# Attention of a gated layer on one core: two Q/K and value buffers, products spread over the heads, weight copies on GpSimd

## What is computed

```python
# 16 heads of 32
scores = einsum("bqhd,bkhd->bhqk", q, k) / sqrt(32); probs = softmax(where(causal, scores, min))
attn = einsum("bhqk,bkhd->bqhd", probs, v).reshape(b, s, d) @ Wo.T
mod = 0.1 * tanh(attn @ A)                       # rank 16
gate = silu(h @ W_in.T + mod * (h @ A) @ B)
out = hidden + (gate * (h @ W_up.T)) @ W_down.T
x = x + tanh(g_ffn) * out
```

## Time and profile before

| | |
|---|---|
| median of 3 runs | 1079.77 us (1079.33 to 1080.65) |
| the profiled execution | 1080.39 us |
| its span | 1078.7 us |
| TensorE matmuls, busy | 1035.0 us (96%) |
| TensorE weight loads | 860.9 us (80%) |
| VectorE | 735.5 us (68%) |
| ScalarE | 613.1 us (57%) |
| GpSimd | 177.7 us (16%) |
| mean granted TensorE clock | 0.997 |

### The profile page before, as it was taken

One profiled execution on the slowest core, in us unless ns is written; L12 is line 12 of the kernel. 1 busy time (PEld: TensorE's weight loads), 2 busy tenths in 40 slices (PEclk: granted clock), 3 DMA queues, 4 the chain that ended last, 5 costly groups with the idle time before them and its releaser, 6 DMA issues.

```text
span 1078.7 us, 17949 instructions
## 1 busy us (share of the span) xinstructions
PE 1035.0 (96%) x5336; PEld 860.9 (80%) x5337; DVE 735.5 (68%) x1662; ACT 613.1 (57%) x1463; POOL 177.7 (16%) x156
## 2 busy tenths in 40 slices
PE   6999999999999999989999999999999999899998
PEld 6787878777888888878888888778888877788887
DVE  7766747996665559985664589966655689854443
ACT  4464547886444458875444378864354588754342
POOL 4536122320000003320000024200000133200000
PEclk9899999999999999999999999999999999999999
DMA  6534132443322425243322354432234342333221
GB/s 244 188 141 165 39 118 70 97 100 120 105 88 90 151 69 140 64 119 128 108 89 88 108 142 97 112 117 88 88 102 141 85 121 68 79 91 105 88 88 49
DMA packets 47063, 115.59 MB, mean 107 GB/s; under 512 B 6800, under 2 KB 6800, under 8 KB 46096
## 3 DMA queue, kind: packets, MB, share of 16 engines
q1 hardware_dynamic: 43968, 105.06, 33.1%
q0 software_dynamic: 3040, 9.96, 2.7%
HBM read 76.46 MB, written 13.37 MB: 83 GB/s over the span
## 4 chain that ended last, share of the span: by engine, by line
PE 80%; DVE 9%; issue 3%; DMA 3%; ACT 2%; SPq 1%; POOL 1%; DVEq 0%; ACTq 0%; POOLq 0%
PE bank L510 64%; PE bank L709 4%; PE bank L722 3%; DVE wr L1326 3%; DVE nb L1338 3%; PE bank L681 3%; DMA stack<-wr 2%; PE bank L758 1%; SPq L307 1%; DVE big L1347 1%; PE bank L685 1%; ACT big L962 1%; PE bank L769 1%; PE bank L566 1%; DMA big<-in_x,gidx 1%
## 5 line engine op out<-in xcount | busy, mean ns | idle before, releaser
L510 PE MATMUL bank<-hT,wr 128*128 128x512 f32 x1488 | 358.4, 390 | 0.0
L510 PEld LDWEIGHTS bank<-hT,wr 128*128 128x128 f32 x1488 | 278.9, 188 | 59.9 <-issue 1.3
L510 PE MATMUL bank<-wr,actr 128*128 128x512 f32 (+1 forms) x1224 | 303.3, 397 | 2.2 <-DVE actr L1308 1.5
L510 PEld LDWEIGHTS bank<-wr,actr 128*128 128x128 f32 x1224 | 229.1, 190 | 51.1 <-issue 3.3
L1376 DVE SCALAR_TENSOR_TENSOR wr<-stream,lns,wr 128x256 fp32r<-128x256 f32 x256 | 122.3, 538 | 51.0 <-ACT wr L1001 51.0
L1326 DVE TENSOR_TENSOR wr<-bank,wr 128x512 fp32r<-128x512 f32 (+1 forms) x224 | 124.6, 600 | 19.7 <-ACT wr L878 19.7
L962 ACT ACTIVATE big<-bank,nb 128x512 f32<-128x512 f32 (+3 forms) x256 | 131.7, 531 | 9.7 <-DVE nb L1338 8.2
L878 ACT ACTIVATE actr<-act_sb 128x512 fp32r<-128x512 f32 x64 | 40.4, 632 | 145.7 <-DVE act_sb L1390 145.7
L878 ACT ACTIVATE wr<-bank 128x512 fp32r<-128x512 f32 (+1 forms) x224 | 102.6, 532 | 27.8 <-PE bank L510 18.7
L1013 ACT ACTIVATE sil<-bank 128x512 f32<-128x512 f32 x64 | 38.1, 596 | 137.6 <-PE bank L758 137.6
L485 POOL TENSOR_SCALAR big<-big,rr 128x256 f32<-128x256 f32 x64 | 78.0, 1219 | 205.9 <-DVE rr L1343 205.9
(11 more groups left out here) (182 smaller groups left out, 1078.6 us busy)
## 6 DMA issues: line engine op xcount, KB each, us to landing
stream<-in_wmlp SPq DMA_DIRECT2D x64, 512.0 KB, 4.0
stack<-wr SPq DMA_DIRECT2D x192, 128.0 KB, 2.3
stream<-in_wmlp SPq DMA_DIRECT2D x64, 256.0 KB, 2.7
big<-in_x SPq DMA_DIRECT2D x4, 1024.0 KB, 5.5
big<-y_rows SPq DMA_DIRECT2D x4, 1024.0 KB, 5.6
residual<-big SPq DMA_DIRECT2D x4, 1024.0 KB, 5.1
big<-residual SPq DMA_DIRECT2D x4, 1024.0 KB, 5.6
out<-big SPq DMA_DIRECT2D x3, 1024.0 KB, 4.5
```

Of the source, the lines that this page charges most:

```text
L510: mm = pe.matmul(dst, lhs(pl, k), rhs(pr, k), start=start and i == 0, stop=stop and i == n - 1, skip_group_check=skip)
```

## The change

- `qk` and `vst` have two buffers, taken by q modulo 2. The high half of Q waits for the stack DMAs of two quads back. In `vst` the high and low halves of two heads lie side by side without zeros, so `attend` loads 48 columns of weights in place of 64, and a memset of the tile goes.
- Each of heads 0 to 8 has six projection products: those of K of quad 1 are half ahead of the loop, and then come Q and K of the later quads by halves.
- Q of quad 1 is split ahead of the loop. In it K of quad q + 1 is split at j = 1, and Q of quad q + 2 at j = 3 of quads 0 and 1. The values of quad q + 1 are split at j = 2 of quad q, those of quad 0 at head 0.
- The weights of quads 2 and 3 are copied by GpSimd (`weights_high`), a projection of 512 columns at a time, and its subtraction follows each copy. ScalarE still copies those of quads 0 and 1 ahead.
- The first up product is spread over heads 9 to 14, two matmuls each, behind `attend`.
- Scores wait for the exponentials bank by bank.
- K of quad 0 goes to bank 3 and the value products of tiles 2 and 3 to bank 6, so that bank 7 can be cleared (the matmul with `zeror`) before the first scores. The last transposes of head 0 wait until bank 6 is read out.
- The loops over quads are written out on every engine.

```diff
@@ -91,11 +93,14 @@
-qk = carve(6144, 2048).rearrange("p (m t) -> p m t", m=4)
-pts = carve(8192, 4 * PACKED).rearrange("p (h a c) -> p h a c", h=2, a=2)
-VS = QH * 64 + 64
-vst = carve(8192 + 4 * PACKED, TT * VS).rearrange("p (t c) -> p t c", t=TT)
-vst_v = vst[:, :, 0:QH * 64].rearrange("p t (h c) -> p t h c", h=QH)
+qk = carve(6144, 4096).rearrange("p (n m t) -> p n m t", n=2, m=4)
+pts = carve(10240, 4 * PACKED).rearrange("p (h a c) -> p h a c", h=2, a=2)
+VS = QH * 2 * R
+vst = carve(10240 + 4 * PACKED, 2 * TT * VS).rearrange("p (n t c) -> p n t c", n=2, t=TT)
+vst_v = vst.rearrange("p n t (g s c) -> p n t g s c", g=2, s=2)
+vp_v = flat[:, 6656:6656 + TT * H * R].rearrange("p (t g c) -> p t g c", t=TT, g=H // 2)
...
@@ -415,6 +420,16 @@
+    def weights_high(b, q, which):
+        pool.wait_ge(qk_done, (b * NQ + q - 1) * 2 + which + 1)
+        g.tensor_copy(wqs[:, HI, which, :, :], wqk_v[:, which, :, q * P:q * P + P]).then_inc(wq_hi, 1)
+    def weights_low(b, q, which):
+        pool.wait_ge(wq_hi, (b * NQ + q) * 2 + which + 1)
+        g.tensor_tensor(wqs[:, LO, which, :, :], wqk_v[:, which, :, q * P:q * P + P],
+                        wqs[:, HI, which, :, :].bitcast(F32), ALU.subtract).then_inc(wq_lo, 1)
...
@@ -485,18 +491,20 @@
-        weights_low(b, 1)
+        for which in range(2):
+            weights_low(b, 1, which)
         normalise(b * H)
         for q in range(NQ):
             for j in range(QH):
                 if q < NQ - 1 or j < QH - 1:
                     normalise((b * NQ + q) * QH + j + 1)
-                if j == 1 and q < NQ - 2:
-                    weights_low(b, q + 2)
+                if j < 2 and q < NQ - 2:
+                    weights_high(b, q + 2, j)
+                    weights_low(b, q + 2, j)
         if b < NB - 1:
-            weights_low(b + 1, 0)
+            for which in range(2):
+                weights_low(b + 1, 0, which)
...
@@ -655,12 +663,10 @@
-            pe.wait_ge(wq_hi, n + 1)
-            pe.wait_ge(wq_lo, n + 1)
-            if which and to == QKB:
-                pe.wait_ge(qk_lo, n * 2 + 1)
+            pe.wait_ge(wq_lo, n * 2 + which + 1)
+            if q:
+                pe.wait_ge(qk_lo, n * 2 + which)
...
@@ -685,17 +688,24 @@
+        if not first:
+            pe.wait_ge(exp_ok, n * 4 - 3)
         rows(3, True)
         mask(0, 3 * P, 1)
+        if not first:
+            pe.wait_ge(exp_ok, n * 4 - 1)
         rows(2, True)
         rows(0, False)
         mask(1, 2 * P, 2)
+        if not first:
+            pe.wait_ge(exp_ok, n * 4)
         rows(1, True)
         mask(2, P, 1)
-    def turn_probs(n, par, first=False):
+    def turn_probs(n, par, first=False, values_out=0):
...
@@ -719,35 +732,35 @@
-                mm = pe.matmul(bank[ATT][0:64, kt * P:S], vst[:, kt, 64 * j:64 * j + 64],
+                at_row = 64 * (j // 2) + R * (j % 2)
+                mm = pe.matmul(bank[ATT][0:3 * R, kt * P:S], vst[:, q % 2, kt, at_row:at_row + 3 * R],
                                pts[:, j % 2, part, at:at + w], start=False, stop=False, skip_group_check=True)
         mm.then_inc(pv_done, 1)
-    def head_step(b, q, j, ahead):
+    def head_step(b, q, j):
         n = (b * NQ + q) * QH + j
-        if j == 2 and ahead == 2:
-            project(b, q + 2, 0, half=0)
-        if j == 0 and ahead:
-            project(b, q + 1, 1)
-        if j == 3 and ahead == 2:
-            project(b, q + 2, 0, half=1)
-        if ahead or j < QH - 1:
+        head = q * QH + j
+        if j == 0 and q < NQ - 1:
+            project(b, q + 1, 1, half=1)
+        elif j and q < NQ - 2:
+            project(b, q + 2, (0, 0, 1)[j - 1], half=(0, 1, 0)[j - 1])
+        if head < H - 1:
             turn_probs(n + 1, (j + 1) % 2)
-        if not ahead and j < QH - 1:
-            if j == 0:
+        if head < H - 3:
+            m = b * (H // 2) + q * 2 + (j + 3) // 2
+            scores(n + 3, (j + 1) % 2, m * 48 + 48)
+        attend(b, q, n, j)
+        if UP_FROM <= head < H - 1:
+            if head == UP_FROM:
                 pe.wait_ge(qk_lo, (b + 1) * (NQ * 2))
                 pe.wait_ge(cg_hi, b * NCH + 1)
                 pe.wait_ge(cg_lo, b * NCH + 1)
-            up_part(0, ((0,), (1,), (2, 3))[j])
-        if ahead or j < QH - 3:
-            m = b * (H // 2) + q * 2 + (j + 3) // 2
-            scores(n + 3, (j + 1) % 2, m * 48 + 48)
-        attend(b, q, n, j)
+            up_part(0, head - UP_FROM)
...
@@ -821,18 +837,12 @@
-        turn_probs(b * H, 0, first=True)
+        turn_probs(b * H, 0, first=True, values_out=b + 1)
         scores(b * H + 2, 0, b * (H // 2) * 48 + 96)
-        pe.wait_ge(vpb_ok, b + 1)
-        pe.matmul(bank[ATT][:, :], zeror[:, :], hT[:, HI, 0, :], start=True, stop=False,
-                  skip_group_check=True).then_inc(pv_done, 1)
-        with pe.Fori(0, NQ - 2) as q:
+        project(b, 1, 1, half=0)
+        for q in range(NQ):
             for j in range(QH):
-                head_step(b, q, j, 2)
-        for q, ahead in ((NQ - 2, 1), (NQ - 1, 0)):
-            for j in range(QH):
-                head_step(b, q, j, ahead)
+                head_step(b, q, j)
...
@@ -968,30 +979,32 @@
-    def head_step(b, q, j, ahead):
+    def values_high_of(b, q):
+        if q < 2:
+            act.wait_ge(vpa_ok, b + 1)
+            act.wait_ge(vpb_ok, b + 1)
+        else:
+            act.wait_ge(pv_done, b + 1 + (b * NQ + q - 1) * QH)
+        copy(vst_v[:, q % 2, :, :, HI, :], vp_v[:, :, 2 * q:2 * q + 2, :]).then_inc(vst_hi, 1)
+    def head_step(b, q, j):
         n = (b * NQ + q) * QH + j
-        if ahead or j < QH - 1:
+        if q < NQ - 1 or j < QH - 1:
             exponentials(n + 1, (j + 1) % 2)
             normalise(n + 1, (j + 1) % 2)
-        if j < 2 and ahead:
-            split_qk(b, q + 1, j)
+        if j == 1 and q < NQ - 1:
+            split_qk(b, q + 1, 1)
+        elif j == 3 and q < NQ - 2:
+            split_qk(b, q + 2, 0)
         for i, (bk, w, at) in enumerate(((4, 512, 0), (5, 512, 512), (6, 256, 1024))):
             act.wait_ge(p_turned, n * 3 + i + 1)
             copy(pts[:, j % 2, HI, at:at + w], bank[bk][:, 0:w]).then_inc(pt_hi, 1)
-        if j == 0:
-            act.wait_ge(pv_done, b + 1 + n)
-            act.wait_ge(vpa_ok, b + 1)
-            act.wait_ge(vpb_ok, b + 1)
-            act.wait_ge(vst_zero, 1)
-            copy(vst_v[:, :, :, 0:R], vp[:, :, bass.ds(q * QH, QH), :]).then_inc(vst_hi, 1)
-    def quad(b, q, ahead):
-        for j in range(QH):
-            head_step(b, q, j, ahead)
-            if j == 1 and ahead == 2:
-                split_wqk(b, q + 2)
+        if q == 0 and j == 0:
+            values_high_of(b, 0)
+        elif j == 2 and q < NQ - 1:
+            values_high_of(b, q + 1)
...
@@ -1467,14 +1480,14 @@
+        qk_low(b, 1, 0)
         maxima(b * H + 1)
         dve.wait_ge(vp_done, b * 2 + 2)
         v.tensor_copy(vp[:, 2:4, :, :].rearrange("p t h r -> p (t h r)"),
                       bank[VALUES[1]][:, :]).then_inc(vpb_ok, 1)
-        with dve.Fori(0, NQ - 2) as q:
-            quad(b, q, 2)
-        quad(b, NQ - 2, 1)
-        quad(b, NQ - 1, 0)
+        for q in range(NQ):
+            for j in range(QH):
+                head_step(b, q, j)
```

96 lines of the change are left out of this document (48 added, 48 removed).

## The result

The changed kernel takes 1064.55 us (median of 4 runs, 1063.31 to 1066.72), the kernel before, on the same chip, 1079.55 (4 runs, 1077.52 to 1080.65). The ratio is 0.9867, with a 95% interval of 0.9854 to 0.9879: faster by 15.0 us, where 1063.0 was forecast. The profiled execution took 1066.72, span 1064.6.

What follows compares the result with a forecast made beforehand. VectorE was taken as the fullest engine in the attention loop, with 3.3 us a batch of waits. Terms 1.06 + 0.94 + 0.65 + 0.60 - 0.22 + 1.15 = 4.2 a batch, some 17 in four, gave 1063.0 us, range 1058.5 to 1071.

Steps and rivals of the forecast that it cites:

- the forecast's own case: Whole kernel: 1060 to 1067 us, the summed gains halved or full; chance 0.60.
- 3.3 us a batch is waiting on VectorE: Attention loop, head 1's to head 15's reciprocal: VectorE's work fills 64.9 of 68.2 us, the rest is waits.
- The second Q/K buffer: First heads of quads 1 and 2: removes two 0.53 waits for ScalarE's Q copy, held by stack DMAs; 1.06 a batch.
- The wait for attend goes: 0.65: Head 12: two value buffers remove VectorE's 0.61 wait for the values' high half, 0.65 a batch with its gap.
- Six products a head ... gives nothing: Heads 0 to 8: TensorE's nine steps make 41.85 us, VectorE's 41.9; level, so the even spread alone gains nothing.
- Q of quad 1 ahead: Before the loop: one Q half-split moves to where VectorE sat idle, gaining 0.60 a batch.
- minus 0.22: Head 1: maxima start 0.60 later, so late exponentials delay its reciprocal by about 0.2, 0.22 with the gap.
- Up products: Behind head 15: last transposes no longer wait behind up products; gate products start 6.0 after the reciprocal, not 7.17; 1.15 gained.
- Loops written out: ... so nothing: Quad loops: heads 8 to 15 already stand outside a loop, and the 4.28 step is one of them; gain 0.
- pass to the end in full: Between batches: all 4.2 us a batch reach the total, as TensorE never idles from gate products to the next scores.
- The level engines: Rival, six-product heads: TensorE and VectorE delay each other, losing 1.4 to 2.2 us a batch; 1067 to 1073, chance 0.24.
- GpSimd's pair: Rival, four steps: weight copy plus subtraction, taken as 2.4 us, holds VectorE from 4.4; at 4.7 costs 5.4 a batch; chance 0.06.

Runs made afterwards that it cites:

- run with the longer pair: Changed kernel with GpSimd's weight subtraction made three times, two of them useless, in four heads a batch: 1079.08 us, ratio 1.0007 to the kernel before.

## Why the prediction was right, and where not

The measured 1064.55 lies in the range and in the forecast's own case (1060 to 1067). Faster was right. The total per batch, 4.2 forecast and 4.7 measured (4.4 without the late stack load of before), was right for a reason that holds: the prediction counted how far VectorE was from being full, and the change filled it. That the time itself came within 1.6 us of 1063.0 is in part luck. Loops and tails gained 1.9 more than the forecast 16.8, of which 1.15 is that one stack load, and this hid part of the 3.4 lost at the branches. The terms of the sum were also wrong one by one, and only their total fits. Step by step:

- **What bounds.** "3.3 us a batch is waiting on VectorE" was right. The loop fell by 3.8, to 64.6 against a forecast 64.9; 0.6 of it is the half of Q that was moved ahead.
- **Split among the parts.** This was wrong as a price list. Undone from the changed kernel, the values are worth 3.00, or 2.7 at full clock (said 0.65), the weight copies 0.33 (said 0.94), the up products 1.45 (said 1.15), the finer waits 0.00 (said 0), the even products with Q's split a head earlier 1.61 (said 0). The second Q/K buffer (said 1.06) was not undone. Its two waits are gone from the trace, but its price stays open. The step that failed is "The wait for attend goes: 0.65": it took the one visible wait as the whole price. The same wait was there in quads 1 and 2, under Q's wait for the stack loads, and would have come out with that one gone. Alone it gives 0.40.
- **"Six products a head ... gives nothing"** was wrong with Q/K in two buffers: a head of twelve makes K's copy late by 0.67, and the step 5.79, in two of its three places. Q's split was moved back in the same run; its step kept the usual 4.88, so little of the 1.61 can be its own.
- **Q of quad 1 ahead.** Not undone by itself. Against the kernel before with quads written out, steps 0 and 1 went from 5.21 and 5.34 to 4.63 and 4.88, but GpSimd's weight copies are in that too. Of the "minus 0.22" for late exponentials 0.03 is seen in the stretch before the fourth loop.
- **Up products.** Right in kind; in the tail 0.85 of it as measured, and 0.56 more in step 13, which the text did not see: before, the values' wait in step 12 covered it. The last transposes came 2.18 behind the reciprocal and not 1.93, and two up products still stand before the last attend.
- **"Loops written out: ... so nothing", and "pass to the end in full".** This failed. The prediction asked whether a written-out head is slower than a looped one, and it is not. It did not ask what the longer body does to the branch at its end: TensorE stood 1.77 and 1.64 us there in the profiled execution, 3.4 of the 18.65 gained. Taking the branch away took the stall away, and writing the quads out, with nothing else changed, brought it to the kernel before.
- **The rivals.** The level engines did not hold each other up: steps 0 to 8 average 4.7, and the plain ones are 4.27. GpSimd's pair takes 2.0, not 2.4 (0.61 and 1.30), so it ended in time and VectorE's scalings kept 1.04; at 4.7 to 4.8 us it decided, as written (from 4.4 on). Its price was 5.4 a batch and measured 3.6, some 0.9 for each of four pairs, where it had counted 1.1 to 1.7. The chance of 0.06 rested on the pair's length, and that held; the argument that an overlap of 0.17 in the earlier trace rows showed no cost did not, since a longer overlap shows one.

## What to carry to other kernels

Waits at the same place stack up: the profile shows the one that ends last, and the price of each part depends on which are already gone. Estimate a bundle by how far the fullest engine is from full, and say of single waits only what they are worth alone or last. When a hardware loop's body is written out further, look at the first instructions behind its branch back and at the instruction queue's packets there, and when an engine that shares the State Buffer with VectorE gets more to do, look at when its work ends.

## What the runs showed of the hardware

**A branch back over a written-out body.** TensorE stood for 1.0 to 1.8 us after each branch back once the quads were written out, and did not with them in a loop of their own (153.15 against 154.16 and more). The instruction queue q8 moved 35 packets, 0.57 MB, in place of 15 and 0.25 MB, and 29 with TensorE's batch loop written out. When the packets move tells more. From 490 to 720 us, which is most of one batch and holds a branch back in the looped kernels, q8 moves nothing in the kernel before. In the changed one, then in the one with TensorE's batch loop written out, it moves:

```profile
q8 instruction: 9, 0.15, 0.3%
```
```profile
q8 instruction: 7, 0.11, 0.2%
```

So before, TensorE went through this batch without a fetch, and with the quads written out every batch is fetched anew. Written out in full it is fetched as well, in order, and there is no stall. The stall therefore goes with the branch and a body that is fetched again, and not with fetching as such. All nine kernels with the quads written out inside the batch loop move 9 packets from the gate products of one batch to those of the next where a branch back lies between. The Trainium skill, Runtime: NRT & Kernel Launch, section Instruction fetch mechanics, says that instructions are fetched ahead in sequence and that a taken branch to a target outside what is held forces a fetch before execution goes on. The traces agree with that, and the price is what they add. By the page TensorE holds 2048 instructions. From which length on a body is fetched again was not measured.

**VectorE and GpSimd on the State Buffer.** In the run with the longer pair one scaling grew from about 0.6 to 1.44 us beside a subtraction of GpSimd that lasted 1.35. GpSimd's own scaling of 256 columns takes 1.02 after VectorE is done (436.04) and 1.23 beside it (446.36). The Trainium skill, SBUF — State Buffer, section Who interferes with whom, states an exclusive lock, under which the later instruction waits for the whole of the first. That there is such a conflict the traces confirm. That the wait is whole they don't: VectorE's second scaling would have waited until 436.06 and then needed some 0.6 more, to 436.7, and it was done at 436.28. Nor does GpSimd's scaling at 446.36 wait for all of VectorE's pair, which ends at 447.34: with its own 1.02 behind that it would end at 448.4, and it ended at 447.59. The profile gives GpSimd's spans only roughly, so this is no measurement of how the two share.
